# GNN kernel on one core: the node features x requested in three parts instead of two, and the remainders of two tiles moved behind group 4

## What is computed

```python
edge_index = jnp.stack([src, dst])
x = _layernorm(x + L0_gnn(x, edge_index, ...), axis=-1)
x = _layernorm(x + L1_gnn(x, edge_index, ...), axis=-1)

def L0_gnn(x, edge_index, eps, W1, b1, g1, be1, W2, b2, g2, be2):
    agg = segment_sum(x[src], dst, num_segments=N)
    h = (1.0 + eps) * x + agg
    h = relu(batch_norm(h @ W1 + b1, g1, be1))      # 512 -> 1024
    h = relu(batch_norm(h @ W2 + b2, g2, be2))      # 1024 -> 512
    return x + h

def L1_gnn(x, edge_index, W1, b1, W2, b2):
    h = relu(x @ W1 + b1) @ W2 + b2                 # 512 -> 256 -> 512
    return h + segment_sum(h[col], row, num_segments=N)
```

## Time and profile before

| | us |
|---|---|
| median of 3 runs | 255.98 |
| lowest, highest | 255.82, 256.71 |
| the profiled execution | 255.75 |
| its span in the trace | 253.9 |
| TensorE busy | 234.4 (92% of the span) |
| VectorE busy | 150.2 (59%) |
| ScalarE busy | 121.3 (48%) |
| GpSimd busy | 93.1 (37%) |
| mean granted TensorE clock | 0.975 of full |

### The profile page before, as it was taken

One profiled execution on the slowest core, in us unless ns is written; L12 is line 12 of the kernel. 1 busy time (PEld: TensorE's weight loads), 2 busy tenths in 40 slices (PEclk: granted clock), 3 DMA queues, 4 the chain that ended last, 5 costly groups with the idle time before them and its releaser, 6 DMA issues.

```text
span 253.9 us, 3833 instructions
## 1 busy us (share of the span) xinstructions
PE 234.4 (92%) x1463; PEld 200.6 (79%) x1463; DVE 150.2 (59%) x354; ACT 121.3 (48%) x213; POOL 93.1 (37%) x80
## 2 busy tenths in 40 slices
PE   0838999999999999999999999999999999999990
PEld 0817998778888888888888888888889986788970
DVE  1679799883965443444444255351606799936373
ACT  0635674664677075554555304060404589115372
POOL 5500000004900008465656303112096499851241
PEclk9975999999999999999999999999999999999997
DMA  3488500000077401111000295000009600000334
GB/s 109 146 257 225 127 3 0 4 0 5 3 271 250 162 3 41 41 41 44 0 0 0 76 187 82 0 3 0 0 15 165 166 3 0 0 0 3 124 124 157
DMA packets 24451, 17.99 MB, mean 71 GB/s; under 512 B 14056, under 2 KB 19213, under 8 KB 24431
## 3 DMA queue, kind: packets, MB, share of 16 engines
q1 hardware_dynamic: 23868, 17.38, 25.0%
q10 hardware_dynamic: 402, 0.20, 0.3%
q0 software_dynamic: 160, 0.13, 0.2%
HBM read 8.51 MB, written 5.92 MB: 57 GB/s over the span
## 4 chain that ended last, share of the span: by engine, by line
PE 76%; DVE 9%; POOL 6%; DMA 5%; ACT 3%; issue 1%; SPq 0%; DVEq 0%; POOLq 0%
PE ps L1142 22%; PE ps L1125 22%; PE ps L1069 17%; PE ps L1194 7%; PE ps L1212 6%; DVE hot_s L749 2%; POOL ul L470 2%; PE ps L1049 2%; DMA src_i<-in_src 2%; DMA pairs<-pair 2%; DMA run<-pairs,start_i 1%; POOL u L468 1%; PE ps L1020 1%; DVE hot_k L752 1%; DVE xl L724 1%
## 5 line engine op out<-in xcount | busy, mean ns | idle before, releaser
L838 DVE BATCH_NORM_STATS2 stats<-ps 128x6 f32<-128x500 f32 (+1 forms) x36 | 21.6, 600 | 48.9 <-PE ps L1125 25.0
L1069 PE MATMUL ps<-AT,xh 128*128 128x500 f32 (+2 forms) x120 | 43.2, 371 | 0.0
L1069 PE MATMUL ps<-AT,xl 128*128 128x500 f32 (+2 forms) x120 | 41.4, 356 | 0.0
L1125 PE MATMUL ps<-h0h,wh 128*128 128x500 f32 (+1 forms) x96 | 33.9, 353 | 0.0
L1125 PE MATMUL ps<-h0h,wl 128*128 128x500 f32 (+1 forms) x96 | 33.9, 353 | 0.0
L1125 PE MATMUL ps<-h0l,wh 128*128 128x500 f32 (+1 forms) x96 | 33.8, 352 | 0.0
L432 POOL TENSOR_TENSOR wl<-w1s,wh 128x512 fp32r<-128x512 f32 x8 | 10.1, 1302 | 47.2 <-ACT AT L507 47.2
L437 POOL TENSOR_TENSOR wl<-w2s,wh 128x512 fp32r<-128x512 f32 x8 | 11.1, 1384 | 43.9 <-ACT wh L609 43.9
L1069 PEld LDWEIGHTS ps<-AT,xl 128*128 128x128 f32 (+1 forms) x120 | 23.2, 193 | 2.7
L1069 PEld LDWEIGHTS ps<-AT,xh 128*128 128x128 f32 (+1 forms) x120 | 23.1, 193 | 2.7
L585 ACT ACTIVATE std<-mv,epsc 128x1 f32<-128x1 f32 x12 | 3.5, 295 | 44.8 <-DVE mv L839 44.8
(11 more groups left out here) (137 smaller groups left out, 509.7 us busy)
## 6 DMA issues: line engine op xcount, KB each, us to landing
turns<-half_out SPq DMA_DIRECT2D x10, 320.0 KB, 2.2
out<-x SPq DMA_DIRECT2D x9, 256.0 KB
w1s<-in_L_gnn_W SPq DMA_DIRECT2D x4, 512.0 KB, 6.0
w2s<-in_L_gnn_W SPq DMA_DIRECT2D x8, 256.0 KB, 2.7
xs<-in_x SPq DMA_DIRECT2D x1, 1280.0 KB, 7.8
xs<-in_x SPq DMA_DIRECT2D x1, 1024.0 KB
lws<-in_L_gnn_W SPq DMA_DIRECT2D x1, 512.0 KB, 5.2
lw2s<-in_L_gnn_W SPq DMA_DIRECT2D x1, 512.0 KB, 3.8
```

The lines of the kernel that those rows point to most:

```text
L838: link(nc.vector.bn_stats(stats[:, 6 * c:6 * c + 6], ps[:, zbank(t, c), 0:c1 - c0]))
L1069: last = mm(o, part[0:r, k, d * P:d * P + P], AT[0:r, k, c0:c1], start=(k == 0 and j == 0), stop=(k == NT - 1 and j == 1))
L1125: last = mm(ps[:, zbank(t, c), 0:c1 - c0], w[:, t, d * P:d * P + P], h[c][:, d, :], start=(d == 0 and j == 0), stop=(d == DT - 1 and j == 2))
```

## The change

x is requested in three parts. `X_FIRST` = 3 tiles (768 KB) go out behind src as before; tiles 3 and 4 (512 KB) are requested only when the store of the packed pairs has landed (`pair_out`), under a semaphore of their own, `x_mid`; tiles 5 to 9 follow behind the gathers as before. On TensorE the turning of tiles 3 and 4 moves behind the turning of `rel`, in front of group 0. On ScalarE `x_high` and `x_turn` of tiles 3 and 4 come behind `x_turn` of tiles 0 to 2. On VectorE `x_low` of tiles 3 and 4 moves from ahead of `rel` to behind the one-hots of group 4.

```diff
+        X_FIRST = 3
+
+        def x_landed(k):
+            return (x_in, 16) if k < X_FIRST else (x_mid, 16) if k < half else (x_in2, 32)
...
-            sp.dma_start(xs[:, 0:half, :], x[0:half * P, :].rearrange("(t p) d -> p t d", p=P)).then_inc(x_in, 16)
+            sp.dma_start(xs[:, 0:X_FIRST, :], x[0:X_FIRST * P, :].rearrange("(t p) d -> p t d", p=P)).then_inc(x_in, 16)
+            sp.wait_ge(pair_out, 16)
+            sp.dma_start(xs[:, X_FIRST:half, :], x[X_FIRST * P:half * P, :].rearrange("(t p) d -> p t d", p=P)
+                         ).then_inc(x_mid, 16)
             sp.wait_ge(runs_asked, 1)
...
-                act.wait_ge(*((x_in, 16) if k < half else (x_in2, 32)))
+                act.wait_ge(*x_landed(k))
...
-            for k in range(half):
+            for k in range(X_FIRST):
                 x_high(k)
-            for k in range(half):
+            for k in range(X_FIRST):
+                x_turn(k)
+            for k in range(X_FIRST, half):
+                x_high(k)
+            for k in range(X_FIRST, half):
                 x_turn(k)
...
-            for k in range(half):
+            for k in range(X_FIRST):
                 x_low(k)
...
+            for k in range(X_FIRST, half):
+                x_low(k)
             v.wait_ge(flag_set, 1)
...
-            for k in range(half):
+            for k in range(X_FIRST):
                 x_cols(k)
             pe.wait_ge(start_set, 2)
             for c in range(2):
...
+            for k in range(X_FIRST, half):
+                x_cols(k)
```

More of the change, by code:

```diff
@@ L214, in gnn_kernel @@
             sem(n) for n in ("dst_in", "src_in", "eps_in_s", "par_in", "lb1_in", "b2_in"))
-        x_in, x_in2, w1_in, lw1_in, lw2_in = (sem(n) for n in ("x_in", "x_in2", "w1_in", "lw1_in", "lw2_in"))
+        x_in, x_mid, x_in2, w1_in, lw1_in, lw2_in = (
+            sem(n) for n in ("x_in", "x_mid", "x_in2", "w1_in", "lw1_in", "lw2_in"))
         w2_in = [sem(f"w2_in{i}") for i in range(W2R)]
@@ L1015, in x_cols @@
                 r = rows[k]
-                pe.wait_ge(*((x_in, 16) if k < half else (x_in2, 32)))
+                pe.wait_ge(*x_landed(k))
                 if k >= half:
```

## The result

The change makes the kernel slower: 257.39 us in the median of 22 runs (255.51 to 258.43), against 255.91 for the kernel before beside them (22 runs, 254.81 to 257.10); the ratio is 1.0044, with a 95% interval of 1.0029 to 1.006 (the two medians alone stand at 1.0058). The runs of the changed kernel fall in two clusters with nothing in between: six from 255.5 to 255.8 and sixteen from 256.8 to 258.4. The profiled execution took 258.08 us, 2.3 more than that of before, so its trace shows a case of the upper cluster. In the experiments, one execution of 340.29 us, in a slower state of the chip, is left out.

The account below looks back on a forecast made before the run. TensorE and VectorE both near their limit from 21 to 38 us, neither alone setting the time. 255.75 - 1.2 (store) + 1.2 (remainders) - 1.0 (waits) = 254.75; median 0.23 above: 255.0 us, range 254.5 to 257.1.

Parts of the forecast that it names:

- The first term: Store of the pairs ahead of the first gather: pair_out, and the gather with it, about 1.2 us earlier.
- the rule of taking turns: DMA engines alternate queues packet by packet, so x could not delay the pairs long; the store would gain far less than 1.2 us.
- so it can start at about 8.8: First gather's start, from start_i's end at 8.49 and 0.3 us behind the store; caps the gain at 1.25 us.
- my bound: Tiles 3 and 4 in flight overlapping the first gather's data: cost at most 0.3 us.
- the price of 0: Cost counted for the first gather's data overlapping the tail of tiles 3 and 4: 0 us.
- the 0.3 us to spare: Slack of the first gather's result before that of the second gather is due: 0.3 us.
- The second term: VectorE behind group 4: two remainders moved there cost 2 x 0.60 = 1.2 us.
- group 5 starts exactly where it does now: VectorE's group 5: 22.42 - 1.2 + 1.2 = 22.4, unchanged.
- The third: Waits that go from build 7 on, with TensorE's clock rising early: -1.0 us at the end.
- so small a gap does not count: TensorE's 0.65 us gap ahead of build 5 leaves the clock rise at 23.2 to 24.8; forecast, 50%.
- rival 1: The gap ahead of build 5 holds the clock back: rise at 26.5 to 28.2, build 7 -0.1 to +0.8 us; 27%.
- rival 2: Store not released: pair_out moves 0 to 0.3 us, group 5 at 23.6, build 5 at 24.8; 256.3 to 257.5; 15%.

Follow-up runs that it names:

- The changed kernel with a dense start: The changed kernel with useless transposes of the identity in all of TensorE's gaps from 12 to 25 us: 255.45 us, ratio 0.9989.

## Why the prediction was wrong

The forecast was 255.0 us and faster, the range ended at 257.1, and the measurement is 257.39 and slower. The sum was -1.2 (store) + 1.2 (two remainders) - 1.0 (waits that go, with the early clock).

**The first term failed, above all at one step.** The store itself was right: 2.77 us against 2.6, for the reason given (3.88 again when tiles 3 and 4 were requested at once), and the worry from the rule of taking turns did not come true. What failed is "so it can start at about 8.8". That took the gather's 0.3 us behind the store for its distance behind `start_i` as well. In the trace of before nothing contradicted it, since there the store came last; the experiments give 1.01 us behind `start_i`, which caps the gain at 0.5. The 0.34 us that the profiled execution shows went at the second gather, the later one: 0.14 us at its issue (1.44 us instead of 1.30, for a reason that no run shows), 0.04 until its `rel` started, and 0.14 at the second turning, which ran at the low level. That last one I had not seen at all: the turning takes 0.47 us in all nine traces with three tiles of x ahead of `rel` and nothing added, and 0.33 in the two with five tiles and the three with useless transposes there. The first gather's data did come 0.3 us late behind tiles 3 and 4 in flight, as my bound had it, and the price of 0 that I gave it held: it used up the 0.3 us to spare. By group 0 the term was 0.0 in these executions, 0.2 counted from src, instead of 1.2.

**The second term was right**: 1.20 us for two remainders, from 22.37 to 23.57. But "group 5 starts exactly where it does now" rested on the first.

**The third had the wrong sign in most runs.** The gap ahead of build 5 came as drawn, 0.53 us against 0.65. Of the 2.25 us at build 7, 0.73 is the late start of build 5 and 1.43 is slot 6 at the low level. I held it likelier (50 to 27) that so small a gap does not count. It can: the level rose near 30.1 in the profiled execution, 5.3 us after build 5, later than the 3.0 to 4.6 after it that rival 1 allowed. That it did so in all sixteen runs of the upper cluster and in none of the six others is likely, but only one of the 22 has a trace. Of the profiled executions of variants that have the gap and no useless transposes, two (255.95 and 255.64 us) are at the full level at builds 6 and 7, and the other four reached it 4.0 to 6.4 us after the start of build 5. The Trainium skill, "TensorE: Matmul & The Clock Gate", Part 1, warns that the same kernel warms up at another point from run to run; these traces agree. The changed kernel with a dense start keeps within 0.5 us from run to run, where the kernel before beside it spreads over 1.9.

**What happened is rival 2 joined with rival 1**: group 5 at 23.57 (rival 2 said 23.6), build 5 at 24.76 (24.8), build 7 at 30.19 (29.4 with the late clock). Its figure for both, +1.5 us, is what the medians give; that is partly luck, since the profiled execution was 2.3 us over and the median depends on how many runs fall in each cluster. I had the mechanism for it wrong, though. It was to come about if the store was not released; the store was, and the gather did not follow. And the two cases together had only the far end of a rival of 15% (0.11 for all times above 257.26), while they need only the gather and the clock.

**What held**: the end moves with build 7 (2.25 there, 2.3 at the end), and so do the builds up to group 24 (61.46 instead of 59.19). w1 was requested at 19.09, 0.12 us earlier, with x and not with build 7, and the later builds kept their lag without it. The transposes of tiles 3 and 4 fit ahead of build 0, which started at 17.84 against 17.86.

## What to carry to other kernels

Before a wait is shortened, find each thing that the released instruction waits for and its own distance behind each: a distance read behind the last one says nothing of the others. Near the start, where TensorE's clock has yet to rise, count a half-microsecond gap not only at its own length but also at what a late rise, where it comes, costs the products behind it, and try a few useless transposes in such gaps: here they took the change's loss away, and gave the kernel before 1.0 us. Work moved off one engine's idle time into the stretch in which it is the limit is not hidden there: the 1.2 us of remainders made group 5 start 1.15 us later, and 0.5 to 0.8 us of it reached the end even with the clock taken out.

## What the runs showed of the hardware that I had not expected

- A gather that GpSimd issues starts 1.01 us behind the VectorE instruction that makes its offsets (8.68 to 9.69; 1.00 to 1.02 in nine variants where the store was earlier), but 0.32 behind a store that lands last.
- A subtraction on GpSimd, 1.2 to 1.6 us long, holds a VectorE instruction beside it up by 0.5 to 1.1 us: `rel` took 1.06 us instead of 0.29, hot_k 1.48 instead of 0.41.
- The clock column can read full through a whole trace while products of one form take 0.41 and then 0.28 us. The durations of one form tell the level.
- The tail of a transfer of 512 KB costs a gather of 125 rows about 0.3 us (2.25 to 2.58 us from the end of its issue to `rel` in eight traces, instead of 2.07 to 2.14 in six).
- The same gap of 0.53 to 0.56 us in TensorE's work leaves the level to rise anywhere from the build behind it (the two traces at 255.64 and 255.95 us) to 6.4 us after its start (the one with the remainders moved alone).
